# Last stage of a fused transformer kernel: a 512 point Hadamard transform split into two 256 point products, with sum and difference on VectorE

## What is computed

```python
def fwht(x):                      # Walsh-Hadamard transform, normalized by 1/sqrt(n)
    ...
def act_quant(x):                 # per token
    scale = 127.0 / clip(max(abs(x)), EPS)
    return clip(round(x * scale), -128, 127) / scale
def h_bitlinear(x, w):
    return act_quant(fwht(x)) @ weight_quant(w).T
gate = h_bitlinear(layernorm(x), w_gate)          # 512 -> 2048
up   = h_bitlinear(layernorm(x), w_up)            # 512 -> 2048
x    = x + h_bitlinear(silu(gate) * up, w_down)   # 2048 -> 512
```

## Time and profile before

| | us |
|---|---|
| median of 3 runs | 700.45 |
| lowest and highest run | 697.09, 703.33 |
| the profiled execution, its own time | 697.15 |
| its span in the trace | 695.3 |
| stages a, b and c, up to the first `gate_up` of stage d | 428 |
| steps 3 to 14 of stage d, each | 15.1 |
| the drain after the last POOL wait, from 650.1 to the end | 45.2 |

### The profile page before, as it was taken

The page is one execution under the profiler, slowest core; times in us unless marked ns, Lnnn a source line. Parts: engine busy times, 40 slices in busy tenths (PEclk is TensorE's granted clock), DMA queues, the critical chain, the costliest instruction groups (busy, mean ns, idle before and its releaser), DMA issues.

```text
span 695.3 us, 12424 instructions
## 1 busy us (share of the span) xinstructions
PE 644.4 (93%) x4086; PEld 375.3 (54%) x4086; DVE 564.9 (81%) x1255; ACT 486.3 (70%) x991; POOL 377.6 (54%) x304
## 2 busy tenths in 40 slices
PE   1689899999999999998999999898999999999996
PEld 0376666666767585853444444454555555445543
DVE  6889898998898777367888965778888888888874
ACT  3757778876877675478888823567787887788834
POOL 2015142524242333267776620089999998999970
PEclk9999999999999999999999999999999999999999
DMA  8980323242334353619999930445577656656611
GB/s 215 239 291 16 92 62 77 70 129 69 70 76 107 83 147 82 244 36 222 314 294 280 245 48 16 91 91 84 99 121 130 114 106 136 133 108 124 116 50 46
DMA packets 173194, 88.21 MB, mean 127 GB/s; under 512 B 150610, under 2 KB 152658, under 8 KB 172116
## 3 DMA queue, kind: packets, MB, share of 16 engines
q1 hardware_dynamic: 167252, 71.94, 46.6%
q10 hardware_dynamic: 3408, 11.27, 4.8%
q0 software_dynamic: 2480, 4.33, 3.5%
HBM read 51.20 MB, written 4.19 MB: 80 GB/s over the span
## 4 chain that ended last, share of the span: by engine, by line
PE 43%; DVE 21%; ACT 12%; issue 9%; POOL 8%; DMA 3%; SPq 1%; POOLq 0%; DVEq 0%; ACTq 0%
PE ps L1874 17%; PE ps L1971 7%; PE ps L1953 6%; PE ps L1889 4%; DVE y_sm L1697 4%; PE ps L1826 3%; POOL arena L594 2%; POOL arena L595 2%; PE ps L2029 2%; DVE ps L1657 2%; ACT arena L1050 2%; ACT arena L1033 2%; POOL arena L517 2%; DVE arena L1670 2%; DVE arena L1671 2%
## 5 line engine op out<-in xcount | busy, mean ns | idle before, releaser
L1874 PE MATMUL ps<-arena 128*128 128x256 f16 x1408 | 159.2, 273 | 3.3 <-DVE arena L1373 2.2
L1874 PEld LDWEIGHTS ps<-arena 128*128 128x128 f16 x1408 | 136.6, 98 | 26.4 <-DVE arena L1373 4.7
L2029 PE MATMUL ps<-arena 128*128 128x512 bf16 x512 | 118.5, 380 | 5.8 <-ACT arena L1002 3.8
L594 POOL TENSOR_TENSOR arena<-arena 128x1024 f32<-128x1024 f32 x44 | 103.8, 2358 | 30.5 <-DVE arena L1671 27.2
L517 POOL TENSOR_TENSOR arena<-arena 128x256 f16<-128x256 f32 x88 | 62.2, 724 | 96.8 <-ACT arena L717 96.8
L595 POOL TENSOR_TENSOR arena<-arena 128x1024 f32<-128x1024 f32 x44 | 104.0, 2363 | 0.0
L2029 PEld LDWEIGHTS ps<-arena 128*128 128x128 bf16 x512 | 47.7, 98 | 65.0 <-DVE arena L1663 8.2
L1889 PE MATMUL ps<-arena 128*128 128x512 f16 x352 | 78.4, 379 | 3.8 <-POOL arena L517 3.8
L710 ACT ACTIVATE arena<-ps,gs 128x256 f32<-128x256 f32 x88 | 41.4, 470 | 49.7 <-PE ps L1874 49.2
L478 POOL TENSOR_TENSOR rstd_a<-ve_a,mhalf 128x1 f32<-128x1 f32 x32 | 19.3, 603 | 86.0 <-DVE ve_a L1159 79.5
L2101 PE MATMUL ps<-arena 128*128 128x512 bf16 x256 | 59.8, 379 | 1.5 <-ACT arena L1080 1.5
(11 more groups left out here) (174 smaller groups left out, 1206.3 us busy)
## 6 DMA issues: line engine op xcount, KB each, us to landing
arena<-in_ctx_t SPq DMA_DIRECT2D x5, 1024.0 KB, 6.7
arena<-in_wg_t SPq DMA_DIRECT2D x16, 256.0 KB, 3.7
arena<-in_wu_t SPq DMA_DIRECT2D x16, 256.0 KB, 3.9
arena<-in_wd_t SPq DMA_DIRECT2D x16, 256.0 KB, 4.3
arena<-in_wu_t ACTq DMA_DIRECT2D x4, 1024.0 KB, 6.1
arena<-in_wd_t ACTq DMA_DIRECT2D x4, 1024.0 KB, 6.2
out_x<-X SPq DMA_DIRECT2D x16, 256.0 KB, 2.5
X<-in_x SPq DMA_DIRECT2D x3, 1024.0 KB, 13.5
```

The costliest lines, as they stand in the source:

```text
L594: nc.gpsimd.tensor_tensor(b[:, :, 0, :], a[:, :, 0, :], a[:, :, 1, :], ALU.add).then_inc(d_bfp, 1)
L1874: last = M(bank(n % 2)[:, 2 * P * i:2 * P * i + 2 * P], W[:, b, c * P:c * P + P], part[:, b, at:at + 2 * P], start=(b == 0 and part is xhT ...
L2029: last = M(bank(2 * (n % 2) + i), d_qT[u][:, b, :], W[:, b, D * n:D * n + D], start=(b == 0), stop=(b == KD - 1))
```

## The change

The Hadamard matrix of 512 is [[H, H], [H, -H]] with H that of 256. PE now multiplies blocks 0 and 1 by H into columns 0 to 255 of the bank, and blocks 2 and 3 by H into columns 256 to 511: still 8 matmuls, now 256 columns wide. ACT gets a new instruction, `front_odd`, that copies the second half out of PSUM to a new SBUF tile, `d_front_sum`; it stands between `odd_evac(k-1)` 1 and `d_silu` 2, and in stage c ahead of `d_round(0, 0)`. In `front_scales` DVE waits for it, adds (first half of PSUM plus the copied half) and subtracts, waits for its own difference, and reduces from SBUF; `d_round` reads SBUF in place of PSUM.

```diff
+        d_front_sum = [cut(30 + 2 * u, 512) for u in range(2)]
...
+        d_odd_r, d_halves = sem("d_front_odd_half"), sem("d_front_halves")
...
                 if at(k, NT - 1):
+                    front_odd(0, 0)
                     d_round(0, 0)
...
+            def front_odd(j, w):
+                act.wait_ge(d_f, j + 1)
+                wait(act, d_fr, j - 1)
+                nc.scalar.activation(d_front_sum[w][:, 2 * P:4 * P], bank(front_bank(j, 1))[:, 2 * P:4 * P], ACT.Copy).then_inc(d_odd_r, 1)
+
             def d_round(j, w):
                 act.wait_ge(d_fsm, 4 * j + 3)
                 wait(act, d_qtp, j)
-                nc.scalar.activation(d_r, bank(front_bank(j, 1)), ACT.Copy, bias=ROUND_HALF,
+                nc.scalar.activation(d_r, d_front_sum[w], ACT.Copy, bias=ROUND_HALF,
                                      scale=f_sm[:, w, 3:4]).then_inc(d_fr, 1)
...
                     odd_evac(k - 1, w, 1)
+                if front:
+                    front_odd(k + 1, w)
                 if mid:
                     d_silu(k, u, 2)
...
                 wait(dve, d_fr, j - 1)
-                V.tensor_reduce(c[0], bank(front_bank(j, 1)), AX.X, ALU.max, apply_absolute_value=True).then_inc(d_fsm, 1)
+                halves, total = bank(front_bank(j, 1)), d_front_sum[u]
+                dve.wait_ge(d_odd_r, j + 1)
+                V.tensor_tensor(total[:, 0:2 * P], halves[:, 0:2 * P], total[:, 2 * P:4 * P], ALU.add)
+                V.tensor_tensor(total[:, 2 * P:4 * P], halves[:, 0:2 * P], total[:, 2 * P:4 * P], ALU.subtract).then_inc(d_halves, 1)
+                dve.wait_ge(d_halves, j + 1)
+                V.tensor_reduce(c[0], total, AX.X, ALU.max, apply_absolute_value=True).then_inc(d_fsm, 1)
...
                 for b in range(KD):
                     for part in (d_xh, d_xl):
-                        last = M(bank(front_bank(j, 1)), part[:, b, :], H512[:, b, :],
-                                 start=(b == 0 and part is d_xh), stop=(b == KD - 1 and part is d_xl))
+                        last = M(bank(front_bank(j, 1))[:, 2 * P * (b // 2):2 * P * (b // 2) + 2 * P], part[:, b, :], H512[:, b, 0:2 * P],
+                                 start=(b % 2 == 0 and part is d_xh), stop=(b % 2 == 1 and part is d_xl))
```

## The result

| | before | after |
|---|---|---|
| median, us | 699.42 (4 runs) | 726.54 (4 runs, 724.69 to 727.54) |
| ratio | | 1.036, 95% interval 1.032 to 1.040 |
| the profiled execution and its span | 697.15, 695.3 | 724.69, 722.7 |
| a full step of stage d (from one front maximum to the next, steps 5 to 13) | 15.11 | 17.16 |

The change makes the kernel slower by 27 us. In this document medians are of all executions, and ratios of the fast ones alone. The first part of the page after, beside the earlier trace rows: PE's busy time fell by 8.3 us, DVE's rose by 12.9 and ACT's by 5.0.

What follows compares the result with a forecast made beforehand. It took a chain of waits through DVE and ACT to bound the kernel: 12 x 2.08 = 25.0 plus 1.4 makes 26.4, on 697.15 gives 723.6, with half of 3.3 towards the median 725 us; range 716 to 734.

Steps and rivals of the forecast that it cites:

- The maximum moves by 2.08 us a step: DVE's front maximum in each full step starts 2.08 us later: 1.30 waiting for ACT's copy, 0.78 added work.
- The lower bound of 1.9: Lowest delay of the maximum per full step, with 0.33 and 0.66 in place of 0.39 and 0.78, and some 0.06 less.
- DVE's wait for its own result costs 0.12 us over the pipelined start: On DVE, the reduction waits for the written difference, so add and subtract cost 0.78 us; without that wait 0.66.
- The reduction and the rounding from SBUF cost what they did from PSUM: Reduction of 512 columns from SBUF 0.66 to 0.72 us against 0.68, no change; `d_round` may differ by some 0.05.
- Nothing comes back within the step: Everything behind the maximum in steps 3 to 14 moves by the full 2.08 us, 25.0 over twelve steps.
- Stage c and steps 0 to 2: 1.4: Before the full steps: 0.78 in step 0, 0.76 in step 1, 0 in step 2, less 0.1 gained in stage c.
- The drain keeps its length: The last stretch, ten POOL instructions without a front, stays at 45.2 us: 0 change.
- PE's 0.87 us are worth nothing in a full step: `d_front` on PE is 0.87 us shorter a tile, but `gate_up` 2 behind it waits for `d_lo` 0 anyway: 0.
- PE would be held at q_turn by the rounding, for 1.1 us: `q_turn` holds PE's queue about 1.1 us in a full step until the rounding is done, at no further cost.
- PE follows DVE and ACT; it doesn't lead them.: In a full step PE's weight loads wait for DVE, 0.48 us at `d_front` and 0.47 at `gate_up` 2.
- It decides from the point where L1610 stands off the chain: Condition for PE setting the period: the front maximum on DVE has slack of at least 2.08 us; forecast had it on the chain.
- rival 2: PE sets the period in full steps, so its 0.87 us comes back every step: 683, 685 by the median; chance 6%.

Runs made afterwards that it cites:

- early_copy: The changed kernel with ACT's copy `front_odd` moved up from behind both `odd_evac`s to right behind `d_hi` 1; 709.30 us against 700.91 before, ratio 1.010.
- wait_only: The kernel before plus ACT's copy at its place and DVE's wait for it, the copy used by nobody; 717.60 us against 700.91, ratio 1.021.
- pe_only: The kernel before with only PE's eight matmuls cut to 256 columns, no add or subtract of the halves; 701.63 us against 700.91, ratio 1.000.
- max_first: The kernel before with DVE's `front_scales` moved ahead of `d_lo` 1; 700.48 us against 700.91, ratio 0.999.
- split_woven: The changed kernel with PE, ACT and DVE reordered, only add and subtract ahead of `d_lo` 1, the maximum behind it; 699.85 us against 700.80 before, ratio 0.998.

## Why the prediction was right, and where it was not

The forecast was 725, the measured median 726.5, slower as forecast.

- *The maximum moves by 2.08 us a step.* Measured 2.05. Its two terms: work 0.78, exactly as early_copy has it (0.33 from add to subtract, then 0.41 plus 0.04: 547.47 + 0.41 = 547.88, start 547.92); waiting 1.30, measured 1.26 in wait_only (DVE's idle time 1.17, and 0.1 that a pipelined start loses). The copy started 0.53 after the first `odd_evac` where the rows of before had let me count 0.66, and its end released the add 0.14 later where I had 0.04; these two nearly cancel. (The lower bound of 1.9 was added up wrong: with the 0.06 that it names it is 1.84.)
- *DVE's wait for its own result costs 0.12 us over the pipelined start.* The three instructions took 0.78 and not 0.66. The Trainium skill (VectorE: DVE Perf Modes, The DRAIN you can't avoid), by which a semaphore between DVE instructions costs nothing extra, would have had 0.12 a step less. The trace doesn't bear that out for a dependent pair: 0.45 from start to start, against 0.34 for the independent add and subtract ahead of it. No run has the same pair with and without the semaphore.
- *The reduction and the rounding from SBUF cost what they did from PSUM.* 0.69 against 0.68, and 0.72 against 0.68; the second is hidden, `d_hi` 2 waits 0.84 behind it.
- *Nothing comes back within the step.* Right: 12 steps gave 24.6, predicted 25.0.
- *Stage c and steps 0 to 2: 1.4.* Measured 1.40 from `d_front(0)` to POOL's first start, and its terms hold: 0.81 in step 0, 1.10 in step 1 of which 0.45 comes back (predicted 0.78, 1.11 and 0.35), 0.06 gained in stage c (predicted 0.1). The other 1.4 ahead of `d_front(0)` belongs to no changed instruction; I had put 1.7 there as half of the distance to the median, by luck about as much.
- *The drain keeps its length.* Right: 45.2 in both.
- *PE's 0.87 us are worth nothing in a full step.* Right, and shown by pe_only.
- *PE would be held at q_turn by the rounding, for 1.1 us.* Wrong in its place. PE waits 1.5 us at `h_product` 2, one instruction earlier, for DVE's `first_stage` 0 (L1686), which stands behind `front_scales` on DVE; when that is done the rounding is too, and `q_turn` has no wait. I had not looked at the semaphore d_bf0 in `h_product`. It cost nothing here, since PE had the room, and POOL's wait was 2.90, as forecast.
- *"PE follows DVE and ACT; it doesn't lead them."* Right. The 15.01 busy us of a full step before hide three pauses, because the recorded end of a matmul lies behind the start of the next one. From `down` at 530.04 to `d_front` at 531.92 it is 1.88 us, and as much from there to `gate_up` 2 at 533.80, where eight matmuls in a row take 1.73 (537.93 to 539.66). With 0.25 more ahead of `gate_up` 0 (539.66 to 540.36 is 0.70 for the eight of `h_product`, which take 0.45 at 537.26) that is 0.55 a step, and PE's own work 14.56. The rows of PE before, beside the earlier trace rows:

```profile
530.04 1.89 PE L2101 MATMUL ps<-arena 128*128 128x512 bf16 x8
...
537.26 0.61 PE L2069 MATMUL ps<-H,arena 128*128 128x128 f16 x8
537.71 0.39 PE L2016 MATMUL ps<-I,arena 128*128 128x128 f16 x4
537.93 1.89 PE L2101 MATMUL ps<-arena 128*128 128x512 bf16 x8
539.66 0.61 PE L2069 MATMUL ps<-H,arena 128*128 128x128 f16 x8
540.36 1.90 PE L2029 MATMUL ps<-arena 128*128 128x512 bf16 x8
```

- *"It decides from the point where L1610 stands off the chain"* (rival 2). The condition isn't the right one. In max_first L1610 is on the chain, but PE's queue releases it (0.57), and there PE's saving did count, 0.34 us a step. What decides is whether `d_front` is on the chain.

What stays open: what split_woven would gain if its last waits went. Its chain of waits runs through DVE and ACT, by way of `d_silu` 3, `y_round` and `d_hi` 3 to `d_lo` 3, where DVE waits 0.74; PE waits 0.62 for `d_turned`. The step less DVE's wait is 14.0, so DVE's own work, expected at 14.3 to 14.6, doesn't hold it. No run shortened that chain.

## What to carry to other kernels

Price a new instruction by its place in the queue, not by its length: a copy of 0.39 us cost 1.26 us a step because its consumer had been ready while three other instructions stood ahead of it, and moving it gave the 1.26 back. When a step repeats, look for the loop of waits that closes on itself from one step to the next; taking work off an engine that isn't on it gives nothing (pe_only). A move that shortens that loop can lengthen another: max_first made one through PE of 15.16 us, and there PE's shorter product was worth 0.34 us a step. And work moved from an engine that follows to one that leads is paid in full there (0.78 a step in early_copy), until the orders are changed so that it falls into waits (split_woven).

## What the runs showed of the hardware

- Two dependent VectorE instructions of 128x256 are 0.45 us from start to start, two independent ones 0.33 to 0.34, both with a recorded length of 0.41 to 0.42.
- The add released by ACT's 128x256 copy starts 0.14 us after the recorded end of the copy (546.60 + 0.39 to 547.13), and 0.13 in wait_only, while `d_lo` released by `d_hi` starts 0.03 to 0.04 after. The chain of waits books 0.05 of it to DVE's queue at the wait itself (L1621). DVE handles four waits in a row there; whether that is the reason was not tested.
- The maximum over 512 columns takes 0.68 to 0.69 us from PSUM (before, wait_only) and 0.69 from SBUF (after).
- Eight matmuls of 512 columns in a row take 1.73 us from start to start of the next group, but are recorded as 1.89; summed over a step of 15.11 us the record shows 15.01 busy, the starts 14.56.
